# Attention and feed-forward layer: the causal mask written into PSUM by ScalarE, and loads and splits of the first head in another order

## The reference

```python
q, k, v = (jnp.einsum('btm,mhd->bthd', x, w) for w in (w_aq, w_ak, w_av))
q, k = _rope(q), _rope(k)
s = jnp.einsum('bihd,bjhd->bhij', q, k) / D_HEAD
mask = (i < j)                       # i: query row, j: key column
s = s - INF_APPROX * mask            # INF_APPROX = 1e30
p = jax.nn.softmax(s, axis=-1)
o = jnp.einsum('bhij,bjhd->bihd', p, v)
r = jnp.einsum('bihd,hdm->bim', o, w_ao)
x = _layernorm(x + r)
h = silu(x @ w1.T * s1) * (x @ w2.T * s2)
h = gelu(h @ h1.T * g1); h = gelu(h @ h2.T * g2)
x = _layernorm(x + h @ w3.T * s3)
```

## Time and profile before

| | |
|---|---|
| median of 3 runs | 1032.31 us (1032.29 to 1032.77) |
| the profiled execution | 1032.38 us, with a span of 1030.5 us |
| mean granted TensorE clock | 0.989 |
| busy, share of the span | TensorE 95%, its weight loads 83%, VectorE 80%, ScalarE 58%, GpSimd 53% |
| busy in 300 to 400 us | TensorE 98.3, VectorE 85.9, ScalarE 65.7, GpSimd 70.4 us |

### The profile page before, as it was taken

One profiled execution on the slowest core, in us unless ns is written; L12 is line 12 of the kernel. 1 busy time (PEld: TensorE's weight loads), 2 busy tenths in 40 slices (PEclk: granted clock), 3 DMA queues, 4 the chain that ended last, 5 costly groups with the idle time before them and its releaser, 6 DMA issues.

```text
span 1030.5 us, 19698 instructions
## 1 busy us (share of the span) xinstructions
PE 983.1 (95%) x5648; PEld 854.9 (83%) x5648; DVE 821.1 (80%) x1787; ACT 593.6 (58%) x1263; POOL 546.6 (53%) x549
## 2 busy tenths in 40 slices
PE   3799999999999999999999999999989999999995
PEld 2688888988888898888888888888878888888884
DVE  5888888888888888888888888888866778586744
ACT  4566666666666666666666666665665252433521
POOL 4776677677766767677667767776672101000000
PEclk9899999999999999999999999999999999999998
DMA  8542323532223233222232322222400000000000
GB/s 280 159 139 63 71 61 75 180 93 62 52 63 76 58 78 99 67 52 62 61 71 61 78 66 52 62 51 64 121 1 1 1 1 21 1 20 0 2 19 21
DMA packets 33868, 66.16 MB, mean 64 GB/s; under 512 B 5521, under 2 KB 7057, under 8 KB 32785
## 3 DMA queue, kind: packets, MB, share of 16 engines
q1 hardware_dynamic: 30976, 58.62, 22.4%
q10 hardware_dynamic: 2832, 6.82, 1.8%
HBM read 24.26 MB, written 7.34 MB: 31 GB/s over the span
## 4 chain that ended last, share of the span: by engine, by line
PE 74%; DVE 11%; issue 6%; POOL 3%; ACT 3%; DMA 2%; DVEq 1%; SPq 0%; ACTq 0%; POOLq 0%
PE psum L327 25%; PE psum L992 17%; PE psum L423 9%; PE psum L413 5%; PE psum L410 5%; PE psum L414 4%; PE psum L965 4%; DVE neg_max L655 3%; POOL probs L761 2%; PE psum L1007 2%; DVE by_sin L682 2%; DVE pT L671 2%; DVE by_cos L684 2%; ACT probs L555 1%; ACT pT L567 1%
## 5 line engine op out<-in xcount | busy, mean ns | idle before, releaser
L761 POOL TENSOR_SCALAR probs<-probs,inv_sum 128x128 f32<-128x128 f32 (+7 forms) x256 | 191.3, 747 | 224.6 <-DVE inv_sum L661 224.1
L567 ACT ACTIVATE pT<-psum 128x512 fp32r<-128x512 f32 (+3 forms) x384 | 174.1, 490 | 133.8 <-PE psum L423 132.0
L327 PE MATMUL psum<-pT,vals 128*128 128x512 f32 (+3 forms) x1152 | 241.5, 350 | 1.0 <-DVE pT L671 1.0
L555 ACT ACTIVATE probs<-psum,neg_max 128x128 f32<-128x128 f32 (+7 forms) x256 | 190.2, 743 | 84.5 <-DVE neg_max L655 82.1
L671 DVE TENSOR_TENSOR pT<-psum,pT 128x512 fp32r<-128x512 f32 (+3 forms) x384 | 201.0, 551 | 30.2 <-ACT pT L567 26.2
L655 DVE TENSOR_REDUCE neg_max<-psum 128x1 f32<-128x128 f32 (+7 forms) x256 | 191.7, 749 | 26.5 <-PE psum L414 25.6
L327 PEld LDWEIGHTS psum<-pT,vals 128*128 128x128 f32 x1152 | 187.5, 189 | 23.1 <-DVE pT L671 1.2
L423 PE MATMUL psum<-ident,probs 128*128 128x128 f32 x1152 | 172.4, 276 | 9.0 <-POOL probs L761 6.3
L992 PE MATMUL psum<-hid,w 128*128 128x512 f32 x768 | 176.6, 390 | 0.0
L766 POOL TENSOR_TENSOR swapped<-by_cos,swapped 128x512 f32<-128x512 f32 x128 | 164.5, 1295 | 14.1 <-DMA swapped<-by_sin 14.1
L992 PEld LDWEIGHTS psum<-hid,w 128*128 128x128 f32 x768 | 143.6, 188 | 29.9 <-DVE value L1271 0.4
(11 more groups left out here) (84 smaller groups left out, 1135.7 us busy)
## 6 DMA issues: line engine op xcount, KB each, us to landing
swapped<-by_sin SPq DMA_DIRECT2D x256, 128.0 KB, 2.3
w_stage<-qk_split SPq DMA_DIRECT2D x30, 256.0 KB, 2.7
wv_stage<-v_split SPq DMA_DIRECT2D x15, 256.0 KB, 2.7
x_split<-ffn_raw ACTq DMA_DIRECT2D x2, 1024.0 KB, 5.3
ffn_raw<-g SPq DMA_DIRECT2D x2, 1024.0 KB, 8.4
x_moving<-x_split SPq DMA_DIRECT2D x2, 1024.0 KB, 5.1
out<-y SPq DMA_DIRECT2D x8, 256.0 KB, 2.0
raw_x<-xT SPq DMA_DIRECT2D x3, 512.0 KB, 11.7
```

Source lines behind the costliest of these rows:

```text
L327: ins = nc.tensor.matmul(out_ap, left[a], right[b], start=first and i == 0, stop=last and i == 2)
L555: nc.scalar.activation(probs[:, ib % 4, :width].rearrange("p (h c) -> p h c", h=halves), score_ps[:, ib % 2, :halves, :half], ACT.Exp, bia ...
L567: nc.scalar.activation(pT[chunk][:, 0, 4 * f:4 * f + n_blocks, (ib % 4) * P:(ib % 4 + 1) * P], bank("t", head[1], nth)[:, :n_blocks * P].r ...
L761: nc.gpsimd.tensor_scalar(p, p, inv_sum[:, n:n + 1], 1.0, ALU.mult, ALU.mult).then_inc(probs_ready[0], 1)
```

## The change

1. The mask matmul goes. ScalarE writes the mask (zeros, and -1e30 above the diagonal in the last 128 columns) into PSUM ahead of the scores (`write_mask`), and the score matmuls accumulate on it. Two matmuls at the start (`scores_opened`) mark the two banks as accumulating. `write_mask` for row i stands in ScalarE's list right behind exp of row i - 2 and waits for it.
2. The cut of a long row is no longer in halves: the masked piece has 256, 256, 384 or 512 columns for rows 4 to 7 (`score_layout`), and stands first in PSUM and in `probs`.
3. Loads: w_q and w_k of two heads, half of rope, mask and ident on SP's queue; x of batch 0, the other half of rope, w_v, w_o and the rest of w_q and w_k on ScalarE's queue; x of batches 1 to 3 on SP's queue behind the first pair's swaps.
4. `x_split` goes. The x of a later batch is split in halves shortly before its use: batch 1 in head 1 (ScalarE and VectorE, steps 5 and 7), batches 2 and 3 in heads 8 and 16 on ScalarE (steps 3 and 5), and in heads 9 and 17 on GpSimd (steps 0 and 1).
5. `save_weights` moves into step 3 of head 0. The low parts of the values' weights and of the other heads' weights move to steps 7 and 0. In the first head VectorE makes some of the rope's sum and low parts.
6. Tiles move: `qk_parts` lies in `rT`, `v_parts` in `ffn_raw`; the first head of a batch copies into `rT` and the memset of `rT` goes; four buffers of `by_sin` and four swap semaphores in place of two.

The diff, cut to its core:

```diff
...
+X_STEPS = (5, 7)
+X_HIGH_STEPS, X_LOW_STEPS = (3, 5), (0, 1)
...
+MASK_COLS = BANK
+
+
+def score_layout(ib):
+
+    width = (ib + 1) * P
+    return width, width if ib < 4 else max(2 * P, width - BANK)
...
-    ident_r = sb("ident_r", [P, P], F32R, outer)
-    mask_r = sb("mask_r", [P, P], F32R, outer)
+    mask = sb("mask", [P, MASK_COLS], F32, outer)
...
+    qk_parts = rT[:, T:].bitcast(F32R).rearrange("p (h k d) -> p h k d", h=H - 2, k=4)
+    v_parts = ffn_raw[:, 3 * T:3 * T + 2 * H * P].bitcast(F32R).rearrange("p (a x) -> p a x", a=2)
+    raw_x = [raw_first[:]] + [ffn_raw[:, b * T:(b + 1) * T] for b in range(B - 1)]
...
+    def score_row(ib):
+
+        width, near = score_layout(ib)
+        first = BANK - near if ib >= 4 else 0
+        return score_ps[:, ib % 2, first:first + width]
+
+    def masked_piece(ib):
+
+        return score_row(ib)[:, :score_layout(ib)[1]]
+
+    def prob_block(ib, jb):
+
+        width, near = score_layout(ib)
+        at = (jb * P + near) % width
+        return probs[:, ib % 4, at:at + P]
...
-            sp.dma_start(raw_w[:, 0], w_q).then_inc(qk_loaded, 16)
-            sp.dma_start(raw_w[:, 1], w_k).then_inc(qk_loaded, 16)
-            sp.dma_start(rope[:], rope_in).then_inc(consts_loaded, 16)
-            sp.dma_start(mask_f[:], mask_in).then_inc(consts_loaded, 16)
-            sp.dma_start(ident[:], ident_in).then_inc(consts_loaded, 16)
-            for b in range(1, B):
-                sp.dma_start(raw_x[:, b], xT[:, b * T:(b + 1) * T]).then_inc(x_loaded[b], 16)
-
-
-            def stage_x_moving(b):
-
-                wait_for_pair(sp, v_projected, PAIRS_OF * (b - 1) - 1, NV - 1)
-                sp.dma_start(x_moving[:, b % 2].bitcast(F32), x_split[b - 2]).then_inc(x_moved, 16)
+            first = slice(0, 2 * P)
+            sp.dma_start(raw_w[:, 0, first], w_q[:, first]).then_inc(qk_loaded[0], 16)
+            sp.dma_start(raw_w[:, 1, first], w_k[:, first]).then_inc(qk_loaded[0], 16)
+            sp.dma_start(rope[:, :, :BANK], rope_in[:, :, :BANK]).then_inc(rope_loaded[0], 16)
+            sp.dma_start(mask[:, MASK_COLS - P:], mask_in).then_inc(masks_loaded, 16)
+            sp.dma_start(ident[:], ident_in).then_inc(masks_loaded, 16)
...
             stage_pair(0, 0)
+            for b in range(1, B):
+                sp.dma_start(raw_x[b], xT[:, b * T:(b + 1) * T]).then_inc(x_loaded[b], 16)
             sp.wait_ge(w_saved, W_SAVED)
             with sp.Fori(1, PAIRS_OF) as hp:
                 stage_pair(0, hp)
-            sp.wait_ge(x_saved, X_SAVED)
-            for base, src in zip(FFN_AT, ffn_weights):
-                sp.dma_start(ffn_raw[:, base:base + src.shape[1]], src).then_inc(ffn_loaded, 16)
             for b in range(1, B):
+                if b == B - 1:
+                    sp.wait_ge(x_low, CHUNKS * B)
+                    for base, src in zip(FFN_AT, ffn_weights):
+                        sp.dma_start(ffn_raw[:, base:base + src.shape[1]], src).then_inc(ffn_loaded, 16)
...
-                for h in range(halves):
-                    dst = score_ps[:, ib % 2, h, :half]
-                    left = [a[:, ib * P:(ib + 1) * P] for a in q]
-                    right = [a[:, h * half:(h + 1) * half] for a in k]
-                    nc.tensor.matmul(dst, left[0], right[0], start=True, stop=False)
-                    if h == halves - 1:
-                        nc.tensor.matmul(dst[:, half - P:], ident_r[:], mask_r[:], start=False, stop=False)
-                    nc.tensor.matmul(dst, left[0], right[1], start=False, stop=False)
-                    last = nc.tensor.matmul(dst, left[1], right[0], start=False, stop=True)
+                left = [a[:, ib * P:(ib + 1) * P] for a in q]
+                width, near = score_layout(ib)
+                if width > near:
+                    split_products(score_row(ib)[:, near:], left, [a[:, :width - near] for a in k], True, True)
+                wait_for(pe, mask_written, head, ib)
+                last = split_products(masked_piece(ib), left, [a[:, width - near:width] for a in k], False, True,
+                                      onto_mask=True)
                 last.then_inc(scores_ready[0], 1)
...
-                if before_first(head) and s == 1:
-
-
+                if before_first(head) and s == 3:
                     pe.wait_ge(vo_loaded, 32)
                     for h in range(H):
-                        last = nc.tensor.matmul(vo_ps[:, h * P:(h + 1) * P], raw_w[:, 2, h * P:(h + 1) * P],
+                        last = nc.tensor.matmul(vo_ps(h // 4)[:, h % 4 * P:(h % 4 + 1) * P], raw_w[:, 2, h * P:(h + 1) * P],
                                                 raw_w[:, 3, h * P:(h + 1) * P], start=True, stop=True)
                     last.then_inc(vo_ready, 1)
-                if before_first(head) and s == NI - 2:
-                    pe.wait_ge(masks_ready, 1)
-                    pe.wait_ge(vo_low, 1)
+                    pe.wait_ge(mask_zero, 1)
+                    pe.wait_ge(masks_loaded, 32)
+                    for masked_bank in (0, 2):
+                        nc.tensor.matmul(psum[:, masked_bank * BANK:(masked_bank + 1) * BANK], mask[:, :P], mask[:],
+                                         start=True, stop=True).then_inc(scores_opened, 1)
+                if is_first(head) and s == 1:
+                    pe.wait_ge(vo_low, 2)
...
+            rest = slice(2 * P, H * P)
+            act.dma_start(raw_x[0], xT[:, :T]).then_inc(x_loaded[0], 16)
+            act.dma_start(rope[:, :, BANK:], rope_in[:, :, BANK:]).then_inc(rope_loaded[1], 16)
             act.dma_start(raw_w[:, 2], w_vT).then_inc(vo_loaded, 16)
             act.dma_start(raw_w[:, 3], w_o).then_inc(vo_loaded, 16)
+            act.dma_start(raw_w[:, 0, rest], w_q[:, rest]).then_inc(qk_loaded[1], 16)
+            act.dma_start(raw_w[:, 1, rest], w_k[:, rest]).then_inc(qk_loaded[1], 16)
...
+            def write_mask(head, ib):
+
+                wait_for(act, exp_done, *earlier(head, ib, 2, NI))
+                near = score_layout(ib)[1]
+                nc.scalar.activation(masked_piece(ib), mask[:, MASK_COLS - near:], ACT.Copy).then_inc(mask_written[0], 1)
...
+                if is_first(head) and s == 3:
+                    save_weights()
                 if before_first(head) and s == 1:
+                    act.wait_ge(masks_loaded, 32)
+                    act.wait_ge(mask_zero, 1)
+                if before_first(head) and s == 2:
+                    high_of_weights(1)
+                if before_first(head) and s == 4:
+                    act.wait_ge(scores_opened, 2)
                     act.wait_ge(vo_ready, 1)
-                    nc.scalar.activation(v_parts[:, 0], vo_ps, ACT.Copy).then_inc(vo_high, 1)
-                if before_first(head) and s == 4:
-                    for b in range(1, B):
-                        high_of_x(b)
-                if before_first(head) and s == NI - 2:
-                    save_weights()
-                if before_first(head) and s == NI - 1:
-                    act.wait_ge(vo_low, 1)
-                    act.wait_ge(x_low, B)
-                    act.wait_ge(masks_ready, 1)
-                if is_first(head) and s == NI - 1:
-                    for b in range(2, B):
-                        save_x(b)
+                    for half in range(2):
+                        nc.scalar.activation(v_parts[:, 0, half * BANK:(half + 1) * BANK], vo_ps(half),
+                                             ACT.Copy).then_inc(vo_high, 1)
+                if odd_of_batch(head, b) and b == 0 and s in X_STEPS:
+                    high_of_x(b + 1, X_STEPS.index(s))
+                if odd_of_batch(step_on(head, 1), b) and b > 0 and s in X_HIGH_STEPS:
+                    high_of_x(b + 1, X_HIGH_STEPS.index(s))
                 if is_first(head) and s == 4:
-                    act.wait_ge(w_saved, W_SAVED)
-                    act.wait_ge(wv_staged, 16)
+                    act.wait_ge(qk_low, 2)
                 if exists(ahead):
                     exponentiate(ahead, (s + 1) % NI)
+                if exists(step_on(head, (s + 3) // NI)):
+                    write_mask(step_on(head, (s + 3) // NI), (s + 3) % NI)
...
+                if is_first(head):
+                    dve.wait_ge(rope_loaded[c], 16)
                 wait_for(dve, qk_projected, head, j)
-                wait_for_swap(dve, old_head, old)
+                wait_for_swap(dve, step_on(head, -1), j)
                 wait_for(dve, rope_low, step_on(head, -1), j)
-                nc.vector.tensor_tensor(by_sin[:, j % 2], projected, rope[:, 1, c * BANK:(c + 1) * BANK],
+                nc.vector.tensor_tensor(by_sin[:, j], projected, rope[:, 1, c * BANK:(c + 1) * BANK],
...
+                if before_first(head) and s == NI - 1:
+                    for half in range(2):
+                        low_of_values(half)
+                    low_of_queries()
+                if is_first(head) and s == 0:
```

(3 more changed lines are left out.)

210 lines of the change are left out of this document (119 added, 91 removed).

## The result

The kernel takes 1040.23 us (median of 6 runs, 1039.1 to 1041.11) against 1032.55 us before (6 runs, 1032.29 to 1033.59). The ratio is 1.0071, with a 95% interval of 1.0061 to 1.0081: slower by 7.7 us. The forecast was 1036, with 1030 to 1044 as its own range and 1018 to 1046 as that of all the rivals together. The profiled execution took 1039.49 us, with a span of 1037.7. One run of a later kernel (all masks by matmul) took 2481.64 us where its eleven others took 1029.49 to 1032.66, and the ratio of that kernel leaves it out.

The account below looks back on a forecast made before the run. A chain through TensorE that leaves it around each head's start, where ScalarE is nearly full, was taken as the bound. Start -6, pairs +9.8, x splits +1 made +4.8 on 1032.31: 1037, rounded to 1036; range 1018 to 1046.

Parts of the forecast that it names:

- TensorE's saving: Mask matmuls removed in two stretches of a pair where TensorE sets the pace: 5 x 0.11 = 0.55 us a pair saved.
- The mask writes: Writes 0, 1 and 2 add 1.31 us in ScalarE's full stretch; 0.83 with value projections and 0.35 without are passed on.
- The pair: An even and an odd head together: +0.63 us, 45.8 to 46.4 us; +9.8 us over 15.5 pairs.
- The start: Loads and head 0: first maximum near 21 us, 9 us sooner, partly given back; -6 us, bounds -10 and -2.
- The splits of x: Batches 1 to 3: two ScalarE copies a batch, one in a full step, plus batch 1's VectorE low parts; +1 us.
- The sum: Whole kernel: -6 + 9.8 + 1 = +4.8 us on 1032.31 gives 1037, rounded down to 1036.
- the rival: In the final rounding from 1037 to 1036, the prediction's wording was a little "towards the lower wait".
- Hidden mask writes: Waits in ScalarE's full stretch take in the three writes; pair 0.55 to 0.88 us shorter, 1014 to 1019; chance 0.24.
- TensorE's 28 us in full: All 256 removed mask matmuls at 0.11 us shorten the kernel: 998, some of it lost 1005; chance 0.06.
- The start did not come to nothing: Rival: saves and x loads make head 2's weights late, 4 to 8 us of idle TensorE; 1041 to 1045; chance 0.14.
- ScalarE worse than taken: TensorE waits for mask_written in rows 1 and 2 too: 1046 to 1052; chance 0.06.

Follow-up runs that it names:

- kernel with both edits: Against the kernel with ScalarE masks of rows 3 to 7 only: later x splits in steps 2 and 3, value weights' two stores issued by SyncE; 1018.94 us.

## Why the prediction was right, point by point

**TensorE's saving.** The term of 0.11 us a mask, at five of sixteen places, was -0.55 us a pair; the runs show -0.53, with 0.31 for three masks and 0.22 for two. The Trainium skill, TensorE: Matmul & The Clock Gate, section "Wait — 56ns, not 53.3ns?", has 56 ns for 128 columns, by which the prediction worked out 0.28. The trace agrees with it for the mask matmul's own time, 0.06 us (335.48 to 335.54). But the product behind it takes 0.17 us before the next starts, where the last one takes 0.12, and the measured 0.11 between the two kernels decides.

**The mask writes.** Three of them were put at 1.31 us of ScalarE; they take 1.44 with values: 0.36, 0.48 and 0.60 us a write, not 0.33, 0.44 and 0.54. What is passed on was put at 0.83 and 0.35, and is 0.86 and 0.42. That the 0.83 came out so near is in part luck: the writes took 0.13 us more than was put, and the gaps of that stretch took in 0.10 more (0.58 where 0.48 stood). The 0.03 us behind the accumulator read was right. That the other five writes are free is shown by the kernel that keeps only them.

The Trainium skill, ScalarE: Activation LUTs, section "Step-by-step: what each stage is for", says that ScalarE reaches PSUM with less delay than SBUF. By that rule, the trace agrees in sign: 602 ns for 512 columns into PSUM, 624 between two SBUF tiles in the same trace (631 before). The 0.02 to 0.03 us are not enough to help.

**The pair.** 46.4 us were forecast, the typical pair is 46.47, or +0.70 over before where +0.63 stood. Over 15.5 pairs it is 10.9 for 9.8.

**The start.** The first maximum was right at 20.8 for 21, and the term was mis-sized: 6 us forecast, 4.6 measured. Part of the miss is in the stores of the value weights. Without them in ScalarE's queue the first exp 6 comes 1.5 us sooner, and some 0.9 of it is left at head 4. The prediction had allowed 1 to 2 us of delay for them, and the idle time ahead of row 4's exponential is 2.71. The rest was not taken apart: rope's half came later than I had put it (first product at 11.23, not 10.5), the first scores sooner (19.88, not 20.4).

**The splits of x.** +1 forecast, 0.8 measured between heads 4 and 31. Their first pair is inside the start's term.

**The sum.** -6 + 9.8 + 1 = 4.8 was forecast, and the span grew by 7.2: 1.4 more at the start, 1.1 at the pairs, 0.2 at the end and 0.2 less for x, within the rounding of these terms. Rounding down towards the rival took another 1.1, and the median of the runs lies 0.7 above the profiled execution. Together (2.4 + 1.1 + 0.7) they are the 4.2 us between 1036 and 1040.2.

**The rivals.** Hidden mask writes fall: the pair is 46.5 and not 45.2. But 45.2 is just what the kernel has whose writes, those of rows 3 to 7, are all hidden. TensorE's 28 us in full never come, even with the writes where they cost nothing; 8 us of them do (1030.65 to 1022.63). The start did not come to nothing, and no row shows head 2's weights late. ScalarE worse than taken falls too: TensorE's matmuls wait 1.9 us for mask writes in the whole trace, all of it ahead of 72 us, and its weight loads 3.6.

## What to carry to other kernels

Price a move from one engine to another by where in the period the instruction will stand, not by the two engines' shares. ScalarE at 58% had room for five of eight masks and none for three, and the same edit was worth -8 or +18 us by which rows it took. To find the full stretch, look in the in-order engine's timeline for the copy that another engine waits for, and for the idle time ahead of it: here that idle time, 0.4 us, was all that could be added at that place for nothing. Then make the edit per row, so that its halves can be measured apart.

## What the runs showed of the hardware

- A ScalarE write from SBUF into PSUM takes what its copies in the other direction take: 281, 388, 496 and 602 ns for 128, 256, 384 and 512 columns, where the kernel before has 276, 387, 491 and 603 out of PSUM.
- A ScalarE instruction that waits for the engine's own accumulator read starts 0.03 to 0.04 us behind its end. What it loses is the overlap, and a write that costs 0.36 us there costs 0.20 behind another copy.
- The two stores of the value weights held ScalarE's queue for 2.43 us. The same two, issued later by SyncE, took 1.22 us (from 37.27, kernel with both edits). Why a store's issue takes twice as long in one of them was not tried.
- TensorE's clock can differ between two traces with nearly the same work: at 44 to 48 us one ran at 1.2 GHz for about 3.4 us, behind a wait of 1.25 us, and one stayed at 2.4 GHz, behind a wait of 1.50 us. Estimated from the two first pairs it cost 1.2 us, as much as the smaller terms that were to be measured. A difference of 1 or 2 us between kernels asks for the granted clock of each stretch.
